# A decoder megakernel: values first, the mask laid under the scores by ScalarE, output projection per batch, FFN in two gaps of each step

## The reference

```python
# 1. gated linear attention with decay, group norm, gate; x + its output; layer norm
# 2. cross attention to 32 context rows per batch; x + its output; layer norm -> x
# 3. six layers, each:
qkv = x @ Wqkv                    # x is token-shifted in its upper 64 features first
q = l2norm(q) * q_scale; k = l2norm(k) * k_scale        # 16 heads of 64
q, k = rotary(q) * scale, rotary(k) / scale
# local attention: windows of 32 queries see 64 keys (their own window and the one before)
sim  = where(mask, -max, einsum('bhwie,bhwje->bhwij', bq, bk2) * 8)
attn = softmax(sim); out = einsum('bhwij,bhwje->bhwie', attn, bv2)
x = x + out @ Wo
xn = layernorm(shift(x)) * g + b
a, gate = split(xn @ W1 + b1); x = x + (a * gelu(gate)) @ W2 + b2
# 4. layer norm of (x + the x that entered stage 3)
```

## Time and profile before

| | us |
|---|---|
| three runs | 2315.33, 2317.48, 2319.54; median 2317.48 |
| profiled execution, its own time | 2324.95 |
| span of the profiled execution | 2323.2 |
| TensorE busy | 2096.4 (90%) |
| VectorE busy | 1434.9 (62%) |
| ScalarE busy | 1291.2 (56%) |
| GpSimd busy | 1122.8 (48%) |

### The profile page before, as it was taken

One profiled execution on the slowest core, in us unless ns is written; L12 is line 12 of the kernel. 1 busy time (PEld: TensorE's weight loads), 2 busy tenths in 40 slices (PEclk: granted clock), 3 DMA queues, 4 the chain that ended last, 5 costly groups with the idle time before them and its releaser, 6 DMA issues.

```text
span 2323.2 us, 75905 instructions
## 1 busy us (share of the span) xinstructions
PE 2096.4 (90%) x33992; PEld 1366.7 (59%) x33992; DVE 1434.9 (62%) x1552; ACT 1291.2 (56%) x1616; POOL 1122.8 (48%) x704
## 2 busy tenths in 40 slices
PE   8999998799999899999999899999999999999975
PEld 4655655366666566666665566666666666566651
DVE  1344444577766667677666676676766766676632
ACT  4444254355656666566556565665656655666552
POOL 1110210376655555556555565555555655556520
PEclk9999999799999999999999999999999999999995
DMA  3000000022223222232222332222222232222210
GB/s 101 1 1 1 2 19 28 17 59 59 73 58 83 71 60 57 57 84 67 72 58 57 78 81 64 51 63 75 75 65 56 61 80 68 68 62 65 56 38 18
DMA packets 81775, 128.17 MB, mean 55 GB/s; under 512 B 17070, under 2 KB 27948, under 8 KB 81324
## 3 DMA queue, kind: packets, MB, share of 16 engines
q1 hardware_dynamic: 81452, 123.32, 20.9%
HBM read 21.55 MB, written 1.05 MB: 10 GB/s over the span
## 4 chain that ended last, share of the span: by engine, by line
PE 62%; issue 13%; DVE 12%; ACT 11%; POOL 1%; DMA 0%; SPq 0%; POOLq 0%; ACTq 0%; DVEq 0%
PE ps L588 11%; PE ps L592 9%; PE ps L699 5%; PE ps L660 4%; PE ps L709 4%; PE ps L414 4%; DVE SS L995 4%; PE ps L668 3%; PE ps L597 3%; PE ps L598 3%; PE ps L634 3%; PE ps L440 2%; DVE work L964 2%; DVE MX L1010 2%; ACT work L876 2%
## 5 line engine op out<-in xcount | busy, mean ns | idle before, releaser
L960 DVE TENSOR_TENSOR work<-ps,work 128x1024 f32<-128x1024 f32 x192 | 235.2, 1225 | 388.9 <-ACT work L871 281.4
L1213 POOL TENSOR_TENSOR work<-work,RL 128x1024 f32<-128x1024 f32 x96 | 182.6, 1902 | 604.5 <-DVE RL L980 604.5
L592 PEld LDWEIGHTS ps<-ident,work 128*128 128x128 f32 x3072 | 350.9, 143 | 182.9 <-issue 153.6
L592 PE MATMUL ps<-ident,work 128*128 128x128 f32 x3072 | 394.3, 277 | 40.9 <-ACT work L876 20.8
L1231 POOL TENSOR_TENSOR work<-work,RS 128x1024 f32<-128x1024 f32 x192 | 361.1, 1902 | 116.3 <-ACT RS L924 116.3
L964 DVE TENSOR_TENSOR work<-ps,work 128x1024 f32<-128x1024 f32 x192 | 233.3, 1215 | 0.0
L1225 POOL TENSOR_TENSOR work<-work 128x1024 f32<-128x1024 f32 x96 | 226.6, 2360 | 13.2 <-DVE work L964 5.9
L1218 POOL TENSOR_TENSOR work<-work 128x1024 f32<-128x1024 f32 x96 | 227.6, 2371 | 4.5 <-DVE work L964 4.5
L588 PE MATMUL ps<-WQ,XS 128*128 128x512 f32 x384 | 216.5, 691 | 11.4 <-POOL XS L1203 4.0
L699 PE MATMUL ps<-work,WO 128*128 128x128 f32 x1536 | 204.6, 283 | 17.4 <-issue 15.6
L995 DVE TENSOR_REDUCE SS<-work 128x32 f32<-128x2048 f32 x96 | 218.5, 2276 | 0.0
(11 more groups left out here) (180 smaller groups left out, 3283.3 us busy)
## 6 DMA issues: line engine op xcount, KB each, us to landing
work<-work SPq DMA_DIRECT2D x576, 128.0 KB
work<-work SPq DMA_DIRECT2D x336, 64.0 KB
WQ<-in_wqkv SPq DMA_DIRECT2D x6, 512.0 KB, 3.8
WK<-in_wqkv SPq DMA_DIRECT2D x6, 512.0 KB, 3.9
WV<-in_wqkv SPq DMA_DIRECT2D x6, 512.0 KB, 3.7
WO<-in_wo SPq DMA_DIRECT2D x6, 512.0 KB, 3.9
work<-ZR SPq DMA_DIRECT2D x48, 64.0 KB
W<-in_w SPq DMA_DIRECT2D x6, 341.0 KB, 4.0
```

The source lines that it names most:

```text
L592: m = nc.tensor.transpose(flat(R)[:, t * 128:t * 128 + 128], src[:, t * 128:t * 128 + 128], ident[:, :])
L960: V.tensor_tensor(h16(cos_part[:, j, :]), h16(flat(src)), rotary_tabs[:, bass.ds(g // 16 * 1024 + (8 * j + n) * 64, 64)].unsqueeze(1).broa ...
```

## The change

The blocks and the operations on them stay. The order within a step is new, and so are some places in PSUM:

- TensorE begins a step with the values of block g-1, then come the queries of block g and the heads. After that there is a first gap for FFN work. Keys are turned before queries. After the scores and the turn of the probabilities there is a second gap for FFN work, and the weighing of values ends the step.
- Bank pair X now holds values, mask and scores; Z holds queries, queries turned and probabilities; Y holds heads, keys and weighed values.
- The mask is copied into PSUM by ScalarE (L904 after) instead of being multiplied there by TensorE.
- The output projection is done once for four blocks, as 8 x 2 passes of 512 columns (L595 after), cut into three parts: slices 0 to 2 at n=2, 3 to 5 and 6 to 7 at n=3. VectorE adds it to x and writes the shifted copy itself.
- The FFN of a batch has its centring and variance at n=0, its three hidden chunks at n=1 and its second product at n=2, one to two steps later than before. The gelu table is loaded by an explicit call after the mask of n=1.
- The sum of squares is taken for queries and keys apart, the keys' one after the row maximum and the difference.
- The closing norms of batches 0 to 2 are moved into the last steps and beside the last FFN pass (`finish`), and there are 99 steps instead of 102.

The diff, cut: TensorE's step, then ScalarE's mask (from `act.wait_ge(values_copied, g)`), VectorE's add (`add_projected`), and TensorE's list behind the last step (`finish`).

```diff
-            def step(g, n, f, a, b, c, d):
...
-                    project(bank_x, w_q, 0, n)
-                    project(bank_x, w_q, 1, n).then_inc(q_projected, 1)
...
-                    for q in range(2):
-                        mm(bank_y[:, q, :].rearrange('p (c k) -> p c k', k=64), ident_bf16[:, :], window_bf16[:, 0 if nb == 0 else 1, :].unsqueeze(1).broadcast_to([PARTS, 8, 64]), start=True, stop=False, skip_group_check=True)
...
-                        m = mm(bank_f[:, 0, 0:128], w_o[:, k, :], heads_t[:, k, :], start=k == 0, stop=k == 7)
...
+            def project_out(f, first, last):
+                if first == 0:
+                    pe.wait_ge(wo_loaded, 16 * (f // 4 + 1))
+                    pe.wait_ge(heads_turned_copied, 4 * f + 4)
+                    if due(f):
+                        pe.wait_ge(gate_gelu, 3 * f)
+                for k in range(first, last):
+                    m = mm(bank_f[:, 0, :], w_o[:, k, :], heads_t[:, k, 128 * (f % 2):128 * (f % 2) + 512], start=k == 0, stop=k == 7)
+                if last == 8:
+                    m.then_inc(attn_projected_out, 1)
...
+            def step(g, n, a, b, c, d, f, fo):
+                if b:
+                    pe.wait_ge(wv_loaded, 16 * ((g - 1) // 16 + 1))
+                    if due(g - 1):
+                        pe.wait_ge(scores_shifted, g - 1)
...
+                    m.then_inc(values_ready, 1)
+                if a:
...
+                    project(bank_z, w_q, 0, n)
+                    project(bank_z, w_q, 1, n).then_inc(q_projected, 1)
+                if d:
+                    pe.wait_ge(heads_copied, g - 2)
                     turn(bank_y, heads).then_inc(heads_turned, 1)
+                if f is not None and n == 0:
+                    centre(f)
+                if f is not None and n == 1:
...
+                    hid(0, bank_f)
+                if f is not None and n == 2:
+                    ffn_project(f)
+                if fo is not None and n == 3:
+                    project_out(fo, 3, 6)
                 if b:
                     pe.wait_ge(k_normed, g)
...
                     turn(bank_y, qk_norm[:, 1, :]).then_inc(k_turned, 1)
...
+                    pe.wait_ge(q_normed, g)
+                    turn(bank_z, qk_norm[:, 0, :]).then_inc(q_turned, 1)
...
+                    project(bank_y, w_k, 1, n).then_inc(k_projected, 1)
                 if b:
+                    pe.wait_ge(k_turned_copied, g)
+                    pe.wait_ge(q_turned_copied, g)
+                    pe.wait_ge(mask_seeded, g)
...
                     m.then_inc(scores_ready, 1)
...
+                if b:
+                    act.wait_ge(values_copied, g)
+                    seed = window_mask[:, 0 if n == 1 else 1, :]
+                    A(bank_x.rearrange('p q (c k) -> p (q c) k', k=64), seed.unsqueeze(1).broadcast_to([PARTS, 16, 64]), ACT.Copy).then_inc(mask_seeded, 1)
                 if f is not None and n == 0:
+                    square(f)
+                if f is not None and n == 1:
+                    nc.scalar.preload_act_table_set(GELU)
...
+            def add_projected(f):
+                dve.wait_ge(attn_projected_out, f + 1)
...
+                parts = ((0, 128, 384), (128, 512, 0)) if f % 2 else ((0, 512, 0),)
+                for first, last, at in parts:
+                    end = min(last, 511)
+                    V.tensor_tensor(ffn_x[0:64, first:last], bank_f[0:64, 0, at:at + last - first], x_all[0:64, xo + first:xo + last], ALU.add)
+                    m = V.tensor_tensor(ffn_x[64:128, first + 1:end + 1], bank_f[64:128, 0, at:at + end - first], x_all[64:128, xo + first:xo + end], ALU.add)
...
+            def finish():
+                f = FFN_PASSES - 1
+                last_variance(0)
+                last_variance(1)
+                last_centre(2)
+                centre(f)
+                last_variance(2)
+                variance(f)
+                pe.wait_ge(ffn_input, f + 1)
+                hid(0, bank_f)
+                pe.wait_ge(ln_done, 10)
+                hid(1, bank_x)
+                pe.wait_ge(ln_inverse, 10)
+                hid(2, bank_z)
+                ffn_project(f)
+                last_centre(3)
+                last_variance(3)
```

602 lines of the change are left out of this document (303 added, 299 removed).

## The result

The changed kernel is slower by 0.4%: median 2325.73 us against 2317.08 us, 20 runs of each in turn. The ratio is 1.0037 with a 95% interval of 1.0022 to 1.0052. The forecast was 2220. One of the 20 runs took 3292.94 us; the ratio leaves such disturbed runs out.

The account below looks back on a forecast made before the run. TensorE was busy 90%, but a loop through all engines set the quiet steps. Gains of 64 us (22 rounds), 6 (start) and 27 (end) sum to 97, giving 2228, or 2220 on the median's scale; range 2165 to 2280.

Parts of the forecast that it names:

- Stops: TensorE's stops inside the weighing of values: 1.7 us a round (four steps) instead of 3.1, bounds 0 and 3.1.
- the start: The eight steps before the 22 steady rounds: about 1 us gained each where GpSimd does not start them, 6 in all.
- the end: Closing normalisations, last output projection, fewer steps and last FFN: 27 us gained in all, bounds 20 and 36.
- rival (4): Stops stay or grow, every burst as dense as before: 72.3 to 74 us a round; counted within the forecast's 0.64.
- The hand schedule: Loop through all engines, n being a step's place in its round: 16.3, 17.6, 19.6, 17.3, sum 70.8 against 72.3 us.
- The clamp: VectorE's 32-column operation after the sum of squares: 0.1 to 0.3 us long in all steps, its 2.1 of waiting gone.
- rival (3): Slower: GpSimd's add still catches the clamp, up to 2.1 us a step, round 78.2, 2346 us; chance 0.06.
- The mask write: ScalarE's write of 1024 mask columns into PSUM each step: taken as 1.0 us, upper bound 2.1.
- Rival (1): Loop takes the gain back through longer hand-overs or mask write: round again 75.4, 2284 us; chance 0.19.
- about 12 stops in the weighing: Sign to look for in the weighing of values: stops about 12 in number and nearer its end.

Follow-up runs that it names:

- e5: Changed kernel with 374 small added matmuls spread over the array's eight quadrants, packet borders kept out of the bursts and the weighing's first products; 2233.0 us, ratio 0.9672.
- e6: Kernel before the change with 354 of the cheap spread matmuls, borders kept out of products 0 to 4 and 99 to 127 of the weighing; 2300.1 us, ratio 0.9955.
- e4: Kernel before the change with 226 small added matmuls ahead of the query projection, meant to keep borders off the weighing after product 98; 2321.0 us, ratio 1.0040.
- e2: Changed kernel with 375 small added matmuls, placed to keep packet borders out of the dangerous part of scores and weighing; 2293.9 us, ratio 0.9923.
- e7: Changed kernel with the queries ahead of the values in the first three steps, on TensorE and ScalarE; 2315.9 us, ratio 1.0032.
- e8: Changed kernel with the mask put under the scores by TensorE again and no mask write on ScalarE; 2311.9 us, ratio 1.0013.
- e1: Changed kernel with TensorE's waits for copied queries and mask moved from directly before the scores to between the key projection's halves; 2296.6 us, ratio 0.9933.
- e3: Changed kernel with 336 small added matmuls, placed so that 97 packet borders fall into the dangerous part of scores and weighing; 2399.0 us, ratio 1.0376.

## Why the prediction was wrong

**The step that failed is the term "Stops".** It put 1.7 us a round, 0.55 of what there had been. The changed kernel has 114 us of them in 1760 us or 23 rounds, 5 a round, and its round is 76.1 instead of 72.5. Even the upper bound, 3.1, was passed. Of the 102 us between the forecast span (97 shorter) and the measured one (4.9 longer), 79 are those rounds, (76.1 - 72.5) x 22, and 25 are the start; the end gives 5 back. My estimate had a part of the cause right (packets of about 253 instructions, a burst longer than two of them). It also took all 3.1 us for stops, while the 40.9 us of the earlier trace rows are 1.8 a round. But above all it let the packets begin with the burst, so that only the tail of a burst could be reached, and so that a shorter burst meant fewer stops. The borders run on through the program instead. A step of 620 to 636 instructions moves them on, and they come to lie anywhere in a burst. What counts is how late the following packet is asked for, and that a wait sets. In the old kernel the second value product and the mask (1.4 us) stand between the scores' last wait and their first product, and the scores have no stop at all, though borders fall on all parts of them. In the new one the waits stand directly ahead of both bursts. The rival (4), "stops stay or grow", was named, and its price, 74 a round, was still 2 too low.

**The loop was right.** The hand schedule counts from one key projection to the next and gave 16.3, 17.6, 19.6 and 17.3 for n=0 to n=3, 70.8 in all. The squares of the keys (L924) follow that projection, so they are the measure for it:

```profile
1077.02 1.02 ACT L924 ACTIVATE work<-ps 128x1024 f32<-128x1024 f32 x1 [0.65 <-PE ps L576]
1096.66 1.02 ACT L924 ACTIVATE work<-ps 128x1024 f32<-128x1024 f32 x1 [1.22 <-PE ps L576]
...
1116.29 1.02 ACT L924 ACTIVATE work<-ps 128x1024 f32<-128x1024 f32 x1 [1.22 <-PE ps L576]
1132.64 1.02 ACT L924 ACTIVATE work<-ps 128x1024 f32<-128x1024 f32 x1 [0.88 <-PE ps L576]
1150.16 1.02 ACT L924 ACTIVATE work<-ps 128x1024 f32<-128x1024 f32 x1 [0.64 <-PE ps L576]
1173.43 1.02 ACT L924 ACTIVATE work<-ps 128x1024 f32<-128x1024 f32 x1 [1.22 <-PE ps L576]
1190.98 1.02 ACT L924 ACTIVATE work<-ps 128x1024 f32<-128x1024 f32 x1 [1.22 <-PE ps L576]
```

The step n=2 from 1077.02 is 19.6 long, n=0 from 1116.29 16.4, n=1 from 1132.64 17.5, and n=3 from 1173.43 17.5. These are the shortest of their kind in the whole loop, 71.0 together, and the median steps are 16.4, 17.5, 19.7 and 17.6. So each of the four forecasts was right within 0.3 us. (The n=2 from 1150.16 has a stop in it and takes 23.3.) A mean round of 76.1 is 5 more, which is what the stops take.

With e5 the round is 72.3, which is the 72.5 of the forecast, though by another way: 71.0, 0.7 for its pads and small waits, not stops. The whole of the order's gain comes out less cleanly. e5 and e6 show it to be worth 56 to 66 us, and the forecast without its gain on stops has 97 - 22 x 1.4 = 66; but the parts differ. From e6 to e5 the rounds give (74.77 - 72.32) x 22 = 54 us, with the difference in pads and stops in it, where the forecast has 33. The start loses 15 where it has 6 gained. The end gives 29, and it has 27. That the sums agree is luck.

**The start was forecast at 6 us gained and lost 19.** The term "start" is the second that failed: I took the gain of the steady steps for the first eight as well. In those the old kernel was short (10.6, 13.2), since half of the work is missing and no loop closes; the new order closes it, values behind the row maximum, and the stops add 12.

**The end was right**: 31.8 us gained against 27, within its 20 to 36.

**Single points.** The clamp is 0.18 us long in 95 of its 96 executions, so rival (3) did not come. The mask write takes 1.036 us, as the square into SBUF had it. The page "ScalarE: Activation LUTs" of the Trainium skill (Step-by-step: what each stage is for) calls ScalarE quicker towards PSUM; against the 1.021 and 1.024 of the two squares of the same 1024 columns, which go from PSUM to SBUF, this trace shows no gain. Rival (1) was near the round (75.4) for the wrong reason: the quiet steps show that no hand-over took the gain. The forecast of about 12 stops in the weighing met 32, and 31 more in the scores.

**What stays open.** Where a packet's wait must stand to do no harm differs. In the old kernel a long wait ahead of the weighing held back the next packet when it stood up to the 44th instruction behind a border (border on product 103 of the weighing), and not from the 46th on (product 102); in the new one it did so up to the 90th (product 84), and in e4 up to about the 58th (product 96). I have no run that explains it. The page "Advanced Engine Details and Errata" of the Trainium skill (Engine Queue Depths) gives TensorE's queue 64 places, which lies between these numbers and accounts for none. Nor is it explained that the last column of e2 and e7 is 17 to 18 us lower than that of the changed kernel, and that e8 has 90.8 us after its last square instead of 85.2.

## What to carry to other kernels

When TensorE shows waits "for issue" inside a group of small matmuls, count its instructions, loads and waits included, from stop to stop; if it is 256, a change of order moves the stops as well as the work, and its time can't be read without them. A stop of up to 2.8 us (e1) comes where a wait on another engine ends less than about 3.4 us before the border in a burst of 11 ns products behind it, so keep slower work of TensorE between the last long wait and such a burst. A few hundred cheap products, shared out so that the borders fall into slow work, can be worth more than the change of order itself: here 374 of them, 21 us of work, made the changed kernel 4% faster.

## What the runs showed of the hardware

- TensorE's instructions come in packets of 256 (16.4 KB), and a packet can be late. It takes about 1.1 us to land, and TensorE goes on 1.2 to 1.6 us later. After a long wait that stands within the first 40 to 90 instructions of a packet, the next one starts about 1.0 us behind the wait's end. Stops, from product to product: 1.63 us on average in the scores, 1.8 in the weighing.
- The same small matmul took 0.144 us when all used one quadrant of the array (54.2 us for 375) and 0.057 when they were spread over eight (21.3 us for 374), though the scores reach 0.022. An entry of about 0.2 us for each group of pads would account for the 0.057; that is my estimate from 374 pads in some 60 groups.
- Two kernels with nearly the same work, e2 and e3 (375 and 336 pads), differ by 4.6%, and the places of the packet borders are the only other difference.
- The granted clock was lower where there were stops, though not in step with them: from 480 to 1000 us its mean was 0.96 in the changed kernel and 1.00 in e5, but 0.98 in e3, which has the most stops. Both rows below are of that stretch (stretch, length, busy time and instructions of TensorE, its loads, VectorE, ScalarE and GpSimd, clock, DMA share, GB/s), the first of the changed kernel, the second of e5.

```profile
480.00:1000.00 520.00, 446.69 (x8314) 268.00 (x8313) 327.31 (x352) 316.44 (x388) 303.68 (x193) 0.96 0.25 62
```

```profile
480.00:1000.00 520.00, 472.17 (x9081) 282.00 (x9064) 351.11 (x376) 339.69 (x416) 325.99 (x207) 1.00 0.26 67
```
